# Four layer norms: two of GpSimd's four small operations move to VectorE

## The reference, cut to what matters

```python
def _ln_t(v, eps=1e-05):
    m = jnp.mean(v, axis=-1, keepdims=True)
    s = jnp.var(v, axis=-1, keepdims=True)
    return (v - m) / jnp.sqrt(s + eps)
...
t = t + _L2_attn_ref(_ln_t(t), ...)
t = t + _L2_ffn_ref(_ln_t(t), ...)
t = t + _L3_attn_ref(_ln_t(t), ...)
t = t + _L3_ffn_ref(_ln_t(t), ...)
```

## Time and profile before

| | us |
|---|---|
| time, median of 3 runs (5043.72 to 5045.41) | 5044.32 |
| the profiled execution, its own time | 5044.79 |
| its span, first to last instruction | 5043.0 |
| PE busy | 4215.2 (84%) |
| DVE busy | 2938.1 (58%) |
| ACT busy | 2179.4 (43%) |
| POOL busy | 1824.4 (36%) |

### The profile page before, as it was taken

The page is one execution under the profiler, slowest core; times in us unless marked ns, Lnnn a source line. Parts: engine busy times, 40 slices in busy tenths (PEclk is TensorE's granted clock), DMA queues, the critical chain, the costliest instruction groups (busy, mean ns, idle before and its releaser), DMA issues. The chain is left out here.

```text
span 5043.0 us, 74851 instructions
## 1 busy us (share of the span) xinstructions
PE 4215.2 (84%) x23003; PEld 1647.9 (33%) x23003; DVE 2938.1 (58%) x5302; ACT 2179.4 (43%) x4008; POOL 1824.4 (36%) x1333
## 2 busy tenths in 40 slices
PE   5399999937899999999999999966999999855513
PEld 2143434325122222222222222223444444443312
DVE  4778878747777767676767677534000000357774
ACT  3332323237166656565656566653343343511400
POOL 1100000027267767676767677871000000210401
PEclk9699999969599999999999999987999999956655
DMA  1265555437422222222222222011000000110504
GB/s 72 50 134 116 120 118 118 99 139 275 62 32 32 32 32 32 32 32 32 32 32 32 32 32 32 8 48 39 0 0 0 0 0 0 59 67 37 200 0 146
DMA packets 178141, 296.64 MB, mean 59 GB/s; under 512 B 43511, under 2 KB 102909, under 8 KB 175373
## 3 DMA queue, kind: packets, MB, share of 16 engines
q1 hardware_dynamic: 149640, 257.12, 22.6%
q10 hardware_dynamic: 23808, 25.17, 1.4%
q0 software_dynamic: 4368, 10.07, 0.7%
HBM read 94.49 MB, written 69.73 MB: 33 GB/s over the span
## 5 line engine op out<-in xcount | busy, mean ns | idle before, releaser
L1638 DVE TENSOR_REDUCE at_mx<-at_side 128x1 f32<-128x512 f32 x2048 | 1294.2, 682 | 417.0 <-PE at_side L1541 406.0
L1712 ACT ACTIVATE at_P<-at_S 128x512 f32<-128x512 f32 x2048 | 1120.4, 600 | 751.6 <-PE at_S L1573 701.9
L1471 POOL TENSOR_TENSOR at_pairs<-at_P 128x2048 f32<-128x2048 f32 x256 | 1159.9, 4531 | 318.2 <-ACT at_P L1712 297.5
L1573 PE MATMUL at_S<-at_qo,at_ko 99*128 99x512 bf16 x2048 | 786.4, 389 | 75.4 <-ACT at_P L1712 74.4
L1541 PE MATMUL at_side<-at_ko,at_qo 96*128 96x512 bf16 x2048 | 789.9, 399 | 44.2 <-DMA at_ko<-qk 23.3
L1989 ACT ACTIVATE ff_hs<-ff_ph,ff_b 128x512 f32<-128x512 f32 x512 | 351.7, 687 | 524.5 <-PE ff_ph L1959 524.5
L1584 PE MATMUL at_num<-at_P,at_rvt 128*32 128x512 f32 x4096 | 552.2, 612 | 0.0
L1959 PE MATMUL ff_ph<-ffn_Y,ff_w 128*128 (+1 forms) x1024 | 525.0, 595 | 8.6 <-DMA ff_b<-in_b_dram 8.6
L1973 PE MATMUL ff_po<-ff_hs,ff_w2s 128*128 128x512 f32 x1024 | 522.8, 592 | 0.0
L2008 DVE SCALAR_TENSOR_TENSOR X<-ff_po,ffn_b2w,X 128x512 f32 (+1 forms) x32 | 24.0, 751 | 823.0 <-PE ff_po L1973 823.0
L819 DVE SCALAR_TENSOR_TENSOR la_dwq<-la_pad,la_taps,la_dwq 128x1024 f32<-128x1024 f32 x384 | 491.5, 1280 | 11.6
(11 more groups left out here) (410 smaller groups left out, 4538.0 us busy)
## 6 DMA issues: line engine op xcount, KB each, us to landing
la_rep<-la_pad SPq DMA_DIRECT2D x512, 162.8 KB, 3.6
qk<-ap_part SPq DMA_DIRECT2D x32, 768.0 KB, 3.7
at_qo<-qk SPq DMA_DIRECT2D x192, 128.0 KB, 4.7
at_ko<-qk SPq DMA_DIRECT2D x192, 128.0 KB, 7.8
n_ln_xs<-X SPq DMA_DIRECT2D x96, 256.0 KB, 2.3
u<-ap_us SPq DMA_DIRECT2D x32, 320.0 KB, 4.0
X<-in_x_dram SPq DMA_DIRECT2D x4, 2048.0 KB, 25.5
proj<-la_y POOLq DMA_DIRECT2D x32, 256.0 KB, 5.0
```

The source lines that it names most:

```text
L1471: g.tensor_tensor(pairs[i % 2][:, :, :], P[a][:, :, :], P[a + 1][:, :, :], ALU.add).then_inc(pair_done, 1)
L1573: pe.matmul(S[n % RING][:, :], ko[u][:, h, j * C:(j + 1) * C], qo[u][:, h, half * CH:(half + 1) * CH], start=True, stop=True).then_inc(s_r ...
L1638: v.reduce_max(mx[:, n // 2, n % 2:n % 2 + 1], side[bank][:, :], AX.X).then_inc(side_saved, 1)
L1712: a.activation(P[k % SLOTS][:, i, :], S[(4 * k + i) % RING][:, :], ACT.Exp).then_inc(p_ready, 1)
```

## The change

Behind its four aggregations DVE signals itself, waits for that signal, multiplies the four means by -1 and adds epsilon to the four variances, in place. POOL keeps the power and the product, and one signal between them. The tiles for epsilon and -1 stay but are no longer read. All four norms are touched.

```diff
@@ vector_stats
         for r in range(4):
             last = v.bn_aggr(self.mv[u][:, r, :], self.st[u][:, r, :])
-        last.then_inc(self.mv_ready, 1)
+        last.then_inc(self.aggr, 1)
+        v.wait_ge(self.aggr, n + 1)
+        v.tensor_scalar(self.mv[u][:, :, 0], self.mv[u][:, :, 0], -1.0, None, ALU.mult)
+        v.tensor_scalar(self.mv[u][:, :, 1], self.mv[u][:, :, 1], EPS, None, ALU.add).then_inc(self.mv_ready, 1)
@@ gpsimd
-        g.tensor_tensor(rstd, self.mv[u][:, :, 1], self.K["eps"][:, :], ALU.add).then_inc(self.gp, 1)
-        g.wait_ge(self.gp, 3 * n + 1)
-        g.tensor_tensor(rstd, rstd, self.K["neghalf"][:, 0:4], ALU.pow).then_inc(self.gp, 1)
-        g.wait_ge(self.gp, 3 * n + 2)
-        g.tensor_tensor(shift, self.mv[u][:, :, 0], rstd, ALU.mult).then_inc(self.gp, 1)
-        g.wait_ge(self.gp, 3 * n + 3)
-        g.tensor_tensor(shift, shift, self.K["negone"][:, :], ALU.mult).then_inc(self.ab_ready, 1)
+        g.tensor_tensor(rstd, self.mv[u][:, :, 1], self.K["neghalf"][:, 0:4], ALU.pow).then_inc(self.gp, 1)
+        g.wait_ge(self.gp, n + 1)
+        g.tensor_tensor(shift, self.mv[u][:, :, 0], rstd, ALU.mult).then_inc(self.ab_ready, 1)
```

More of the change, by code:

```diff
@@ L1022, in __init__ @@
         self.staged = [m.sem(f"ln_staged{u}") for u in range(r)]
-        self.front_ready, self.stat, self.mv_ready, self.gp, self.ab_ready, self.xt_ready, self.back_ready, self.saved = (
-            m.sem("ln_" + x) for x in ("front_ready", "stat", "mv_ready", "gp", "ab_ready", "xt_ready", "back_ready", "saved"))
+        self.front_ready, self.stat, self.mv_ready, self.gp, self.ab_ready, self.xt_ready, self.back_ready, self.saved, self.aggr = (
+            m.sem("ln_" + x) for x in ("front_ready", "stat", "mv_ready", "gp", "ab_ready", "xt_ready", "back_ready", "saved", "aggr"))
     def sync(self, sp, n, u):
```

## The result

The change takes 5057.37 us (median of 9 runs, 5053.93 to 5060.18) where the kernel before takes 5044.04 (median of 9, 5039.84 to 5046.38): a ratio of 1.0026, 95% interval 1.0016 to 1.0036. It is slower, by 8 to 18 us, and lies 0.2 from the predicted time. The experiments confirm the side, the place and the price of a step, and not the reason for that price.

The account below looks back on a forecast made before the run. DVE was taken to set n2 and n3, ACT n4 and PE the preparation. At +0.32 per step, n2 +7.1 and n3 +6.2 gave +13.3 on 5044.32: 5057.6 us; overall range 5049 to 5068, the forecast's own 5054 to 5065.

Parts of the forecast that it names:

- hand-over: DVE, each chunk: first new operation starts 0.03 after the four aggregations end (0.38), where the copy had started at 0.30.
- DVE's issue work for the copy: DVE in n2 and n3: behind a wait this work has less to hide under, so 0.05 was added per step.
- The lower bound: DVE, each chunk: hand-over, then two operations and the copy 0.08 apart; copy at 0.57 instead of 0.30, +0.27.
- +6.2: n3's total growth: 28 steps from 57.35 to 62.8, +5.5, and the fill, +0.7.
- The fill: Start of n2 and n3: four more additions of 0.32, less the first copy's wait for PE, 0.54: +0.7 each.
- n4's cover: n4: DVE's four steps become 9.05, under ACT's 9.42 for four chunks; 0.37 to spare, so no growth.
- POOL's removal at nothing: POOL, each chunk: two of four operations gone, at least 0.40 of work, counted as no gain beside DVE's 1.87 step.
- In series: Rival, n2 to n4: each new operation waits its predecessor out, +0.49 per step, sum +26.4, 5070.7; chance 0.11.
- Absorbed: Rival, n2 and n3: turns' issue work runs under the new wait, addition 0.27, +6.2, 5050.5, or less; chance 0.26.
- POOL's pace: Rival, n2 to n4: POOL's shorter chain gives back 9.7 in n4 and DVE's additions are hidden, 5034.6; chance 0.04.
- The shared port: Rival, n2 to n4: new DVE operations wait for POOL's to end, 0.5 on 56 steps, +28 more, 5086; chance 0.02.

Follow-up runs that it names:

- written-out copies: The change with VectorE's 32 steps of n2 to n4 written out in place of its loop: 5051.9 us, 1.0016 of the kernel before.
- four additions: The changed kernel with two more VectorE additions behind its two, on tiles nothing else reads or writes: 5062.3 us, 1.0036 of the kernel before.
- both halves: Kernel before with only VectorE's wait and additions (5059.7 us, 1.0031), or with only GpSimd cut to power and product (5038.8 us, 0.9989).
- wait alone: Kernel before with VectorE waiting for its own aggregations ahead of its next instruction, no additions: 5056.7 us, 1.0028 of the kernel before.
- second profile: The kernel before profiled again with no edit: 5044.2 us, 1.0001 of the kernel before.
- wait alone, written out: Kernel before with VectorE's wait for its aggregations, no additions, its steps of n2 to n4 written out: 5047.6 us, 1.0005 of the kernel before.
- behind the copy: The changed kernel with a chunk's wait and two additions put behind the next copy out in n2 to n4: 5049.5 us, 1.0011 of the kernel before.

## Why the prediction came out

**Right in place and price.** n2 and n3 carry the loss; n4 and the preparation moved by 0.2. The step was forecast at 2.19, between 2.14 and 2.25, and is 2.20; the turns at 2.5 to 2.7 are 2.57 to 2.64. The first addition starts 0.03 behind the last aggregation and takes 0.17.

**Wrong in what the price is made of.** The step that failed is this: 0.11 for the hand-over, 2 x 0.08 for the additions and 0.05 for "DVE's issue work for the copy". The issue work is 0.20, not 0.05, and the additions, lying beside it, add 0.01, not 0.16. The lower bound, 0.27, is nearly what the written-out copies show, where there is no register work: 0.56 behind the first aggregation, where it is 0.30 without the change. The sum was right because the two errors cancel, which is luck: the reason given, that the pair carries no wait inside, "which puts it near the lower end", weighed the wrong thing.

**n3 was misread.** The prediction took the copy at 4429.11 for the 29th; it is the 30th. The last four of the 32 copies in the kernel before are these:

```profile
4427.63 0.67 DVE L1089 COPY gqa_Y<-n_ln_back 128x512 f32<-128x512 f32 x1
4429.11 0.69 DVE L1089 COPY gqa_Y<-n_ln_back 128x512 f32<-128x512 f32 x1 [0.81 <-PE n_ln_back L1044]
4431.07 0.69 DVE L1089 COPY gqa_Y<-n_ln_back 128x512 f32<-128x512 f32 x1 [1.27 <-PE n_ln_back L1044]
4433.03 0.69 DVE L1089 COPY gqa_Y<-n_ln_back 128x512 f32<-128x512 f32 x1 [1.27 <-PE n_ln_back L1044]
```

So the 28 steps, from 4371.76 to 4427.63, were 55.87, not 57.35, and n3 came out 1.5 too cheap: by its own terms +7.7, not +6.2. Measured is +9.0. The rest is five turns, which now stand 0.41 above a step in place of the 0.30 that the earlier trace rows gave, and the last three copies, which took 5.89 in place of 5.40 and which the prediction left out. n2, forecast at 63.7 for its 28 steps, took 63.50; its turns stand 0.38 above a step, not 0.48.

**The fill** was put at +0.7 and measured +0.6 in n2 and n3, and +0.9 in n4, where ACT's pace takes it back.

**The total.** With n3 mended the sum would have been 14.8; the stages show 16.3, the medians 13.3, and their interval is 8 to 18. That the time agrees with the forecast to 0.2 is luck within that interval. Against n2 and n3 as they were with the change in the preparation and n4 only, the stages show 19.1, so the loss is not known to better than some 3 us.

**n4's cover** was thin and held. Two turns of ACT in n4 after, against the earlier trace rows:

```profile
4715.00 1.50 ACT L1082 ACTIVATE n_ln_xt<-n_ln_front,n_ln_ab 128x128 f32<-128x128 f32 x4 [1.22 <-POOL n_ln_ab L1073]
...
4724.43 1.50 ACT L1082 ACTIVATE n_ln_xt<-n_ln_front,n_ln_ab 128x128 f32<-128x128 f32 x4 [1.21 <-PE n_ln_back L1044]
```

They lie 9.43 apart, with the same gap whoever is named. It held up to 9.32 of VectorE's work for four chunks (four additions); beyond that it was not tried.

**POOL's removal at nothing** holds for the change. By itself it is worth 0.54 at the start of each norm, which the prediction saw only as slack for the additions.

**The rivals.** "In series" falls: the additions follow each other at 0.04 to 0.08 while each takes 0.14 to 0.17, so the rule of the Trainium skill that it leaned on ("VectorE: DVE Perf Modes", section "The DRAIN you can't avoid") does not describe these operations. The same section of the Trainium skill excepts a next operation that is not held back, which starts earlier; the prediction left that out, and these rows agree with it. "Absorbed" falls: nearly every step is 2.20, above PE's 2.06, and the turns' issue work did not go under the wait but came behind it (turns 2.57 to 2.64). "POOL's pace" falls by both halves. "The shared port" does not act in n2 to n4 and does in the preparation, where idle time hides it (below).

## What to carry to other kernels

Price a wait on the engine that sets the pace by what no longer runs ahead of it: in this loop the next instruction's register work came behind the wait, and that was 0.20 of 0.33 and more than both operations that the wait was for. Two costs in one place need not add: try each alone before summing them. Of all that was tried here, writing that engine's loop out was worth most.

## What the runs showed of the hardware

**Register work and waits.** In the loop the first of the copy's two register instructions starts 126 ns before the last aggregation, or, with a wait ahead of it, 188 ns behind that aggregation's start. The Trainium skill, "Perfetto Trace Analysis", section "Per-engine timelines", says that an instruction of the sequencer's own waits in the sequencer, which decodes the next one only afterwards, while the wait of a VectorE instruction is spent in a queue and the sequencer goes on. With the wait alone, which sits on the first register instruction, the trace agrees (88 and 103 ns one behind the other). In the change the wait sits on the first addition, and the register work still didn't start until 16 ns behind that addition's start. Why it didn't go on during that wait stays open.

**The shared port.** Instructions on the means and variances after, in n2 to n4 and in the preparation (ns of one, min/median/max):

```profile
L1062 DVE TENSOR_SCALAR n_ln_mv<-n_ln_mv x96: 169/170/172, 3367.7 to 4754.9; 128x4 f32<-128x4 f32 x96
...
L1062 DVE TENSOR_SCALAR ap_ln_mv<-ap_ln_mv x32: 169/331/338, 1091.8 to 1244.2; 128x4 f32<-128x4 f32 x32
```

The same operation takes twice as long in the preparation. The timeline of one chunk there:

```profile
1163.31 2.27 POOL L1163 TENSOR_TENSOR ap_part<-ap_left,ap_part 128x512 bf16<-128x512 f32 x2 [1.16 <-ACT ap_part L1257]
...
1165.28 0.33 DVE L1062 TENSOR_SCALAR ap_ln_mv<-ap_ln_mv 128x4 f32<-128x4 f32 x1
1165.53 0.16 DVE L1063 TENSOR_SCALAR ap_ln_mv<-ap_ln_mv 128x4 f32<-128x4 f32 x1
```

POOL's subtractions end at 1165.58 and the addition at 1165.61: it ends with them, as the copy of the earlier trace rows did. Of the 32 additions of this line in the preparation, 28 took 326 to 338 ns, and each of them ended 24 to 27 ns behind a subtraction; the four that took 170 had no subtraction beside them. The prediction had thought that this could happen here, and that it would be hidden.

**TensorE's clock and the step.** The mean granted clock in n2 and n3, as a share of 2.4 GHz, was 0.82 and 0.83 before (0.80 and 0.89 in the second profile), 0.73 and 0.70 after, and 0.93 in both for the kernel before with the steps written out. PE does the same transposes in all of these. A longer step of VectorE mostly goes with a lower clock, but not strictly: 0.77 and 0.80 at 1.99 (wait alone, written out), 0.81 and 0.84 at 2.02 (behind the copy). A slow PE also lengthens steps, and no run separates the two.
